# A fused decoder layer: score banks of PSUM as two interchangeable pairs, a rewritten unit order, and the last expert tile split in halves

## The reference

```python
# x, ctx: (8, 256, 256); 2048 tokens in all
x = _layernorm(x + self_attention(x))         # latent K/V (rank 64) and Q (rank 128),
                                              # content part 16 + rotary part 32 per head, causal softmax, @ W_o
x = _layernorm(x + cross_attention(x, ctx))   # q = x, k = v = ctx, heads of 16, full softmax, @ W.T + b
# experts: 8 experts, top 2 of a softmax gate
gate_probs = softmax(x @ Wg + bg)
topk_probs, topk_idx = top_k(gate_probs, 2);  topk_probs /= topk_probs.sum()
h = gelu(x @ W1[e] + b1[e], exact);  y = h @ W2[e] + b2[e]      # 256 -> 1024 -> 256
x = _layernorm(x + sum over the two chosen experts of weight * y)
```

## Time and profile before

| what | us |
|---|---|
| median of three runs | 747.67 |
| the profiled execution, its own time | 746.01 |
| span inside it | 744.2 |
| PE busy | 623.2 (84%) |
| PEld busy | 453.2 (61%) |
| DVE busy | 514.3 (69%) |
| ACT busy | 399.4 (54%) |
| POOL busy | 286.7 (39%) |

### The profile page before, as it was taken

The page is one execution under the profiler, slowest core; times in us unless marked ns, Lnnn a source line. Parts: engine busy times, 40 slices in busy tenths (PEclk is TensorE's granted clock), DMA queues, the critical chain, the costliest instruction groups (busy, mean ns, idle before and its releaser), DMA issues.

```text
span 744.2 us, 22691 instructions
## 1 busy us (share of the span) xinstructions
PE 623.2 (84%) x8063; PEld 453.2 (61%) x8064; DVE 514.3 (69%) x1106; ACT 399.4 (54%) x847; POOL 286.7 (39%) x245
## 2 busy tenths in 40 slices
PE   3778889889999999888867677689999999999940
PEld 2456656666766666555644445667777777777720
DVE  6898789777866777546667764677766666666635
ACT  4345766667576574575865556344444444444414
POOL 3988454324555441511111010332444444454422
PEclk9899999999999999999997799799999999999985
DMA  8426551140403203213243014311222232222326
GB/s 274 118 65 172 160 165 37 46 142 11 106 3 100 59 13 121 70 37 80 77 152 89 27 57 142 114 31 30 45 44 45 45 52 42 42 42 42 49 41 208
DMA packets 39839, 59.45 MB, mean 80 GB/s; under 512 B 6768, under 2 KB 27504, under 8 KB 39632
## 3 DMA queue, kind: packets, MB, share of 16 engines
q1 hardware_dynamic: 32272, 48.12, 21.9%
q0 software_dynamic: 7488, 10.23, 8.5%
HBM read 34.08 MB, written 11.67 MB: 61 GB/s over the span
## 4 chain that ended last, share of the span: by engine, by line
PE 55%; issue 14%; DVE 13%; DMA 7%; ACT 6%; SPq 3%; POOL 1%; ACTq 1%; DVEq 0%; POOLq 0%
PE bank L1670 7%; PE bank L1272 4%; PE bank L1298 4%; PE bank L1672 4%; PE exp_scores L1323 3%; PE bank L1660 3%; DVE mxc L1062 3%; PE bank L1251 2%; PE max_scores L1660 2%; ACT probs L725 2%; PE bank L1662 2%; PE max_scores L1662 2%; PE max_scores L1661 2%; PE bank L1661 2%; PE bank L1252 2%
## 5 line engine op out<-in xcount | busy, mean ns | idle before, releaser
L725 ACT ACTIVATE probs<-exp_scores 128x768 f32<-128x768 f32 (+1 forms) x128 | 117.5, 918 | 118.5 <-PE exp_scores L1329 56.2
L615 POOL DMA_INDIRECT acc_rows<-x,slot_row x39 | 65.0, 1666 | 131.6 <-DVE x L1178 128.6
L1670 PE MATMUL bank<-w_sb,wp 128*128 x312 | 109.9, 380 | 1.6 <-DVE wp L1165 1.6
L1062 DVE TENSOR_REDUCE mxc<-max_scores 128x4 f32<-128x1024 f32 x64 | 78.1, 1221 | 38.2 <-PE max_scores L1343 38.0
L1672 PE MATMUL bank<-w_sb,wp 128*128 x312 | 85.0, 273 | 0.0
L794 ACT ACTIVATE probs<-bank,b_sb 128x128 f32<-128x128 f32 x152 | 43.5, 370 | 66.2 <-PE bank L1662 66.2
L794 ACT ACTIVATE probs<-max_scores,b_sb 128x128 f32<-128x128 f32 x160 | 45.6, 369 | 60.8 <-PE max_scores L1662 60.7
L1027 DVE TENSOR_REDUCE mx<-max_scores 128x6 f32<-128x768 f32 x64 | 61.0, 952 | 23.9 <-PE max_scores L1311 23.3
L1163 DVE CAST wp<-probs 128x512 f16<-128x512 f32 x78 | 33.8, 433 | 62.2 <-ACT probs L794 61.9
L1272 PE MATMUL bank<-probs,w_sb 128*32 128x256 f32 x768 | 57.3, 402 | 9.4 <-ACT probs L725 7.8
L1660 PE MATMUL max_scores<-xT,w_sb 128*128 128x128 f16 x320 | 61.3, 223 | 2.4 <-DVE xT L1157 2.4
(11 more groups left out here) (263 smaller groups left out, 1730.2 us busy)
## 6 DMA issues: line engine op xcount, KB each, us to landing
w_sb<-w_sb SPq DMA_DIRECT2D x192, 64.0 KB, 2.1
wstage<-in_w_exp SPq DMA_DIRECT2D x16, 512.0 KB, 4.2
w_sb<-in_w_exp SPq DMA_DIRECT2D x8, 512.0 KB, 4.9
wp<-in_w_exp SPq DMA_DIRECT2D x8, 512.0 KB, 3.8
x_sb<-in_x_by_feature SPq DMA_DIRECT2D x8, 256.0 KB, 3.6
x_res<-in_x SPq DMA_DIRECT2D x8, 256.0 KB, 3.0
ctx_raw<-in_ctx SPq DMA_DIRECT2D x8, 256.0 KB, 3.1
x_rows<-x SPq DMA_DIRECT2D x8, 256.0 KB, 2.7
```

The lines of the kernel that those rows point to most:

```text
L615: nc.gpsimd.indirect_dma_start(out=acc_rows[:, :], out_offset=bass.IndirectOffsetOnAxis(ap=slot_row[:, n:n + 1], axis=0), in_=yb[n % 2], i ...
L725: nc.scalar.activation(probs[:, 2 * (k % 2):2 * (k % 2) + 2, 0:cols], ps_e[:, :, 0:cols], ACT.Exp, scale=(SELF_SCALE, CROSS_SCALE)[a]).the ...
L1062: nc.vector.tensor_reduce(mxc[:, 2 * k:2 * k + 2, :], ps_m[:, :, :].rearrange("p h (a k) -> p h a k", a=2), axis=AX.X, op=ALU.max).then_in ...
L1670: mm(o[:, 0:2 * D], ah[:, u, f, :], weights(e, at, 2 * D), start=(f == 0), stop=(f == FC - 1), skip_group_check=True)
```

## The change

**Two interchangeable pairs.** `exp_scores` and `max_scores` become `scores0` and `scores1`, two pairs of banks of the same shape. A fifth table, SCORE_PAIRS, gives for each use in PE's order (`sm`, `cm`, `st`, `se`, `ce`) the pair that it takes. PE waits for the reader of the last use of that pair, whichever kind it was. A stack takes the first bank of a pair. The number of places in `probs` stays four.

**All five orders are new.** Every list is rewritten. Two lines of TENSOR_ORDER stand here for all of them, at about the same place in the program.

**Other banks.** The transposed cross maxima go from bank 0 to bank 2, the cross output projection from bank 1 to bank 0, the gate's ranks from bank 3 to bank 2, its slots and first table from bank 2 to bank 3.

**The first expert tile.** Its transposition (`ft`), its high part (`fh`) and low part (`fl`) become units of the written orders and use bank 0. `ft` stands before the last logits.

**The last expert tile.** DVE weighs the tile before it between its two halves, and PE's `down` steps wait for each half apart.

```diff
 TENSOR_ORDER = """
-... cm7.7 gs1.4 cn.7 ce0.7 cw.6 ce1.7 cv0.7 ce2.7 ce3.7 gs2.4 cv1.7 ce4.7 ce5.7 cv2.7 ce6.7 x2.6 ce7.7 gs3.4 cv3.7 co.7 cb.7 gs4.4 cw.7 gf.4 lg.6 x2.7 lg.7
+... cw.6 cm7.7 gs1.4 cn.7 ce0.7 ce1.7 ce2.7 cv0.7 ce3.7 gs2.4 cv1.7 ce4.7 ce5.7 x2.6 ce6.7 cv2.7 ce7.7 gs3.4 cv3.7 co.7 lg.6 cb.7 gs4.4 cw.7 gf.4 x2.7 ft.4 lg.7
+SCORE_PAIRS = """
+0101010101010101010101010101010101010101010101010101010101001010 ...
+"""
+def pairs_in_turn():
+    uses = [x for x in order(TENSOR_ORDER) if x[0] in ("self_max", "cross_max", "stack", "self_exp", "cross_exp")]
+    return {use: int(bit) for use, bit in zip(uses, SCORE_PAIRS.replace("\n", ""))}
...
-        ps_e = stack.enter_context(nc.psum_tensor("exp_scores", [P, 2, 512], F32))
-        ps_m = stack.enter_context(nc.psum_tensor("max_scores", [P, 2, 512], F32))
+        ps_p = [stack.enter_context(nc.psum_tensor(f"scores{i}", [P, 2, 512], F32)) for i in range(2)]
...
-        ps_rank = [ps_x[3], bank[1]]
-        ps_slots = [ps_x[2][:, 0:2 * P], bank[1][:, T:T + 2 * P]]
-        ps_fin = [ps_x[2], bank[1]]
+        ps_rank = [ps_x[2], bank[1]]
+        ps_slots = [ps_x[3][:, 0:2 * P], bank[1][:, T:T + 2 * P]]
+        ps_fin = [ps_x[3], bank[1]]
-        ps_max = [ps_x[i] for i in (2, 0)]
+        ps_max = [ps_x[i] for i in (2, 2)]
-        ps_out = [ps_x[i] for i in (0, 1)]
-        ps_sh = [ps_m[:, i, :].bitcast(F16) for i in range(2)]
+        ps_out = [ps_x[i] for i in (0, 0)]
+        ps_first = ps_x[0]
...
-            def exps_free():
-            def maxima_free():
+            held = [None, None]
+            def pair_free(i):
+                if held[i]:
+                    once(*held[i])
...
                 elif u == "cross_exp":
-                    exps_free()
+                    pair_free(pair[u, k, b])
                     pe.wait_ge(v_mT[1], b + 1)
...
-                    at[u] = b * (H // 2) + k + 1
+                    held[pair[u, k, b]] = a_p[1], b * (H // 2) + k + 1
...
+                elif u == "first_slots":
+                    bank0_free()
+                    slots_in(0, 0, 16, ps_first)
...
-            slots_in(0, 0, 16)
             for n in range(FIRST):
...
# DVE, the last expert tile
-            tile(N_TILES - 1, 0, False)
+            split_hidden(N_TILES - 1, 0, 0)
             weigh(N_TILES - 2, 1, (N_TILES - 3) * 16)
+            split_hidden(N_TILES - 1, 0, 1)
             weigh(N_TILES - 1, 0, (N_TILES - 2) * 16)
...
# PE, the last expert tile
-            pe.wait_ge(v_al, 2 * N)
-            for f in range(FC):
-                down(0, f, last_at)
+            for half in range(2):
+                pe.wait_ge(v_al, 2 * N - 1 + half)
+                for f in range(4 * half, 4 * half + 4):
+                    down(0, f, last_at)
```

More of the change, by code:

```diff
@@ L1300, in project_heads, with self_max_part @@
                 last.then_inc(pe_w[a], 1)
-            def self_max_part(h, part):
-                hp, rows, s = h // 2, slice(QK * (h % 2), QK * (h % 2) + QK), ps_m[:, h % 2, :]
+            def self_max_part(h, part, b):
+                hp, rows, s = h // 2, slice(QK * (h % 2), QK * (h % 2) + QK), ps_p[pair["self_max", h // 2, b]][:, h % 2, :]
                 q, key = qk16[rows, hp, 0, 0:T], qk16[rows, hp, 0, T:2 * T]
@@ L1330, in self_exp_part, with cross_exp_part @@
                           start=False, stop=half == 1, skip_group_check=True)
-            def cross_exp_part(h, part):
+            def cross_exp_part(h, part, b):
                 hp, r, t = h // 2, QK * (h % 2), part // 2
-                rows, s = slice(r, r + QK), ps_e[:, h % 2, t * T:(t + 1) * T]
+                rows, s = slice(r, r + QK), ps_p[pair["cross_exp", h // 2, b]][:, h % 2, t * T:(t + 1) * T]
                 if part % 2 == 0:
@@ L1503, in _ @@
                         for h in (2 * k, 2 * k + 1):
-                            last = self_max_part(h, part)
+                            last = self_max_part(h, part, b)
                     last.then_inc(pe_max[0], 1)
-                    at[u] = b * (H // 2) + k + 1
+                    held[pair[u, k, b]] = v_max[0], b * (H // 2) + k + 1
                 elif u == "self_negate":
@@ L1519, in _ @@
                         for h in (2 * k, 2 * k + 1):
-                            last = self_exp_part(h, part)
+                            last = self_exp_part(h, part, b)
                     last.then_inc(pe_t[0], 1)
-                    at[u] = b * (H // 2) + k + 1
+                    held[pair[u, k, b]] = a_p[0], b * (H // 2) + k + 1
                 elif u == "cross_exp":
-                    exps_free()
+                    pair_free(pair[u, k, b])
                     pe.wait_ge(v_mT[1], b + 1)
@@ L1603, in _ @@
                         for h in (2 * k, 2 * k + 1):
-                            last = cross_max_part(h, t)
+                            last = cross_max_part(h, t, b)
                     last.then_inc(pe_max[1], 1)
-                    at[u] = b * (H // 2) + k + 1
+                    held[pair[u, k, b]] = v_max[1], b * (H // 2) + k + 1
                 elif u == "x2_transpose":
@@ L1640, in _ @@
             pe.wait_ge(v_rows, 1)
-            def slots_in(n, u, loaded):
-                pe.wait_ge(g_ld[u], loaded)
-                for c in range(DC):
-                    last = nc.tensor.transpose(bank[0][:, c * P:(c + 1) * P], xg[u][:, c * P:(c + 1) * P], ident)
-                last.then_inc(pe_ft, 1)
             w_bytes = w_sb[:, :].bitcast(mybir.dt.uint8)
```

267 lines of the change are left out of this document (137 added, 130 removed), and 3 rows, old and new, of the table UNITS.

## The result

The changed kernel takes 720.4 us (median of four runs, 717.42 to 722.5), beside 746.53 us for the kernel before on the same chip (median of four): a ratio of 0.965, with a 95% interval of 0.960 to 0.969. It is faster. The gain is 26 us where 17.9 were forecast. The time lies inside the range of 716 to 744. The profiled execution has a span of 717.9 us, 26.3 less than before.

A forecast was written before the change was run, and what follows sets the result against it. It saw PE's small holes in its full stretches and an 80 us tail where no engine is full; -5 - 6 - 5.5 - 0.5 - 0.9 = -17.9 us, so 730 us predicted, range 716 to 744.

The forecast's parts named there:

- the likeliest case: Whole run: the forecast itself, 730 us from a sum of -17.9 us, given a chance of 0.50.
- the second rival: Whole run: new order fills PE's other holes too; interleaved part gains -15 us instead of -5, 720 us, chance 0.17.
- The interleaved part: Start to 394 us: pairs remove a third of PE's 15.0 us of waits for score readers, -5 us.
- The maxima: Second term, last batch, 401.35 to 434.93 us: `ge` leaves DVE's path (3.7), PE's maximum waits overlap (2.3), -6 us.
- The exponentials: Last batch, 434.93 to 457.17 us: PE's waits for ACT go, DVE's 15.6 us chain is longest, -5.5 us.
- Into the experts: 457.17 to 473.86 us: first tile's work saves up to 3 us, gathers hold the root about 2, -0.5 us.
- The end: Last expert tile: weighing between its halves starts POOL's last scatters earlier; the last waits for a landing, -0.9 us.
- The start: Before the first batch: reordered loads and one POOL operation less, taken as 0, bounds -1.2 and +3.6 us.
- The pairs are worth nothing: Score banks: the four places for probabilities are the limit, not the banks; -7.1, or 740.6 us, chance 0.18.
- the two readers hold each other up: Interleaved part, batches 1 to 6: each wait is the later of two queues; +18 instead of -5, 753 us, chance 0.07.

The follow-up runs named there:

- Kernel 10: The changed kernel with PE's products of probabilities and values up to two places further ahead in its list, except the last cross-attention: 752.38 us, ratio 1.007.
- Kernels 1 and 4: 1: changed kernel's new lists, pairs given by kind again, 860.49 us; 4: the kernel before with its old lists, pairs used in turn, 756.59 us.
- kernel 12: The kernel before with only `ge` (choice of first tiles' experts, DVE) moved behind the copy of the last batch's transposed maxima: 749.37 us, ratio 1.002.
- Kernel 3: The changed kernel with pairs by kind only for stacks, maxima and exponentials of the last batch's cross-attention: 738.69 us, ratio 0.987.
- kernel 6: The changed kernel with `ge` (choice of first tiles' experts) back ahead of the last batch's fifth cross maximum on DVE: 725.45 us, ratio 0.975.
- kernel 8: The changed kernel with cross-attention's last inverse root ahead of the gathers on POOL, as before: 721.58 us, ratio 0.968.
- kernel 7: The changed kernel with the old end: both halves of the last expert tile split before the weighing, last down steps behind both: 720.71 us, ratio 0.967.
- kernel 5: The changed kernel itself, unaltered, run again: 719.42 us, ratio 0.965.
- kernels 4 and 9: The kernel before, old lists, pairs in turn: 4 everywhere, ratio 1.013; 9 only for the last batch's cross-attention, ratio 1.001.
- kernels 8 and 11: 8 has its own line; 11: changed kernel, one expert piece's ACT rounding and DVE split moved behind the last batch's exponentials, 724.84 us, ratio 0.968.

## Why the prediction came out as it did

*The direction and the range* were right; the likeliest case, 730, was 9.6 us too slow. The sum missed in its first two terms, and some of its reasons were wrong even where the number was not. That 720.4 is also the 720 of the second rival is luck: that rival has its other 10 us in the interleaved part alone, and they came about half there (4.9) and half in the maxima (4.0).

*The interleaved part (forecast -5, measured -9.9).* The failed step is "What the pairs can remove is PE's wait for the reader of scores": the term held nothing else. At the three kinds of unit that it counted (self exponentials, both maxima) the waits for readers fell from 15.0 to 10.1 us, as forecast. But the stacks gave back 2.5 of it (2.9 to 5.4), so all waits for readers fell by 2.8 us. Most of the gain is in PE's waits at the other banks, -12.6 us, which the sum did not hold at all. Cross-attention's products now stand 4.3 units of PE's list behind their last exponential's scores, 3.4 before. Kernel 10 shows that such distances can carry this much: one or two places nearer cost 28 us. That they do carry the 9.9 is read from the waits and not shown by a run of its own. The 9.9 itself comes from one execution each; the other ends of this part in the table would make it 7 to 11. Kernels 1 and 4 show that neither half of the change can be priced alone: against the kernel before, the new lists without the pairs lose 116 us of this part, the pairs without the lists 18. What the pairs buy is the freedom to set units side by side; the lists spend it.

*The maxima (-6, measured -10.0).* `ge` was not on the path in the kernel before (kernel 12: 0 instead of -3.7). PE was, at the lower clock: its product took 1.93 us and its two groups of one-hot sums 3.05 and 3.39, where the changed kernel has 1.07, 1.99 and 1.99 (3.39 and 1.07 stand in the earlier trace rows). That is 3.3 us of PE's path. Kernel 3 shows what the turns hold: with the turns taken out the stretch is 11.6 us longer, of which PE is busy 6.8 us more for the same instructions. The sum priced waits and work at the clock of the kernel before, and did not allow for a higher one. The changed kernel's profiled execution is one of the two shortest in this stretch: five executions with the same instructions there took 23.6 to 26.4 us (last section), so the gain is 7.2 to 10.0 us. How it divides between clock and waits is not settled beyond that.

*The exponentials (-5.5, measured -5.3).* Right in size, wrong in the bound, so the size was luck. DVE's chain of 15.6 us was to be the longer one. With 3.1 us less of it on DVE (11.0 instead of 14.1 us busy, kernel 6) the stretch is the same to 0.01 us. ACT and PE bound it, and their rounds were mis-sized: 3.80, 3.72 and 3.79 us instead of 3.4, and 4.8 from the last pair of exponentials to the reciprocal. Two exponentials take 1.92 us and not 2 x 1.16, a wait that was read as a length; left out were the next scores behind the product (0.60 us) and, in two rounds, the gate weights in ACT's list.

*Into the experts (-0.5, measured -0.9).* The size is right. The gathers took 2.5 us of POOL and not 3.8, so they held the root by 0.9 us and not 2. Their new place is worth 1.9 us (kernel 8), which I had counted only as a cost.

*The end (-0.9, measured -0.1 in all).* The term itself is right: from the third scatter from the end to the last one it takes 9.06 us, 10.03 before. The last scatter is released by DVE, where I said a landing. From the first expert matmul to that third scatter the changed kernel needs 2.1 us more (237.6 against 235.5), and behind the last scatter 1.2 us less (23.5 against 24.8). Ahead of that scatter PE waits for the last gather:

```profile
678.75 0.44 PE L1413 MATMUL scores<-tab,x_sb 128*128 128x128 f32 x2 [0.99 <-DMA x_sb<-x_rows,slot_row]
```

But kernel 7, whose instructions are the same to that scatter, waits 0.76 us there and needs 236.5 us, and kernel 5 needs 237.3. So the stretch is 1.0 to 2.1 us longer than before, and the cause stays open.

*The start (0)* and the moved banks were not tried by themselves; they are inside the first 9.9 us.

*The rivals.* "The pairs are worth nothing" was right of the pairs put into the old lists: 1.001 and 1.013. The rule of the Trainium skill that I set beside it ("TensorE: Matmul & The Clock Gate", section "HAM oscillation", double-buffering PSUM gave that kernel no further gain) agrees with kernels 4 and 9 and disagrees with the changed kernel, in which taking the turns out of 20 uses costs 18 us. "The new order fills PE's other holes too", 720 us with a chance of 0.17, is what happened in the interleaved part, at two thirds of its price. Of "the two readers hold each other up", the sign was PE's waits at exponentials for DVE's maxima: they come to 2.7 us in the changed kernel, spread over nine waits, and the part got shorter all the same.

## What to carry to other kernels

Buffers and the order of work are one change: a second buffer in a list made for one buffer can cost time, and a list made for two can't be judged by the waits of the one. Before a stretch is said to be bound by the engine whose work is removed, look for an idle row of that engine inside the stretch. Where it waits there for another by about as much, the work may be covered, and a run that moves only this work tells it (kernels 12 and 6). And a unit that waits in an in-order list costs its wait once for itself and again for all that stands behind it: give a consumer enough units between it and its producer (here some four; at 2.8 and 2.9 this kernel lost 28 us), and keep cheap work where it fills a wait that stays.

## What the runs showed of the hardware

Kernel 8 has the instructions of the changed kernel in the maxima stretch, and took this for it:

```profile
389.90:416.30 26.40, 21.89 (x189) 13.85 (x180) 22.40 (x56) 17.75 (x31) 2.09 (x1) 0.81 0.10 36
```

The granted clock was 0.81, where the changed kernel's window above has 1.00, and the stretch is 2.8 us longer. In both, PE had waited 2.44 us for ACT ahead of the stacks. In kernel 8 (first row) the sixteen transposes behind that wait took 1.87 us, most of them at the lower of the two levels (1.2 GHz), and in the changed kernel (second) 1.05 us at 2.4 GHz:

```profile
397.18 1.87 PE L1613 MATMUL scores<-ident_h,w_sb 128*128 128x128 f16 x16 [2.44 <-ACT probs L741]
```

```profile
398.76 1.05 PE L1613 MATMUL scores<-ident_h,w_sb 128*128 128x128 f16 x16 [2.44 <-ACT probs L741]
```

So after the same wait the clock fell in one execution and not in the other. Five profiled executions have the same instructions in this stretch: the changed kernel and kernel 7 took 23.6 us at 1.00, kernel 5 24.8 at 0.93, kernels 8 and 11 26.4 at 0.81. Up to 2.8 of the 10.0 us of the second term are this, and nothing in the lists differs between them there.

The exponentials' stretch had a clock of 1.00 in all eight executions with the new lists and the pairs in turn there, and took 16.91 or 16.92 us in each. Between two anchors of such a stretch a change of 0.1 us can be told, which medians of whole runs can't show under 4; in the stretch of the maxima it can't.
